# Value gate folded into a scaled matrix and three LayerNorm chains moved to GpSimd, in an attention and routed-FFN layer

## The reference, cut to what matters

```python
h    = layernorm(x) * (1 + scale_a) + shift_a          # modulation rows from silu(c) @ wmod
q, k, v = h @ Wq.T + bq, h @ Wk.T + bk, h @ Wv.T + bv
p    = softmax(causal(abs(q @ k.T) / 16))
x2   = x + gate_a * (p @ v @ Wo.T + bo)
h2   = layernorm(x2) * (1 + scale_b) + shift_b
tile = argmax routing of h2 over 8 clusters x 8 tiles (sigmoid, piecewise linear in 8 knots)
comp = tanh(gelu(h2 @ w1 + b1) @ w2 + b2)              # 2 numbers per token
mag  = small spline of comp with the parameters of the chosen tile
y    = h2 + mag * directions[tile] * output_scale
out  = x2 + gate_b * (layernorm(y) * gamma + beta)
```

## Time and profile before

| | |
|---|---|
| Median of 3 runs | 475.73 us (473.7 to 475.93) |
| Profiled execution | 474.78 us, span 473.0 us |
| TensorE busy | 403.7 us (85%), 2136 products |
| VectorE busy | 400.6 us (85%), 1367 instructions |
| ScalarE busy | 295.5 us (62%), 645 instructions |
| GpSimd busy | 42.7 us (9%), 64 instructions |
| Mean granted TensorE clock | 0.939 of full |

### The profile page before, as it was taken

How to read it: one execution, slowest core, us unless ns; L and a number is a source line. 1 busy time by engine, 2 the same in 40 slices (tenths; PEclk the granted TensorE clock), 3 DMA queues, 4 the chain that set the end, 5 groups by cost and what they waited for, 6 DMA issues and landing times.

```text
span 473.0 us, 7756 instructions
## 1 busy us (share of the span) xinstructions
PE 403.7 (85%) x2136; PEld 315.1 (67%) x2136; DVE 400.6 (85%) x1367; ACT 295.5 (62%) x645; POOL 42.7 (9%) x64
## 2 busy tenths in 40 slices
PE   2595799999999998999899989998999999963330
PEld 2563568767886886779586858786878787863330
DVE  4436536478799999999999999999999989998986
ACT  2230274949885968597758776797669865772410
POOL 2000003000000022001300040004000400040040
PEclk9879799999999999999999999999999999987565
DMA  8602102100300051104210320024101100110022
GB/s 303 148 2 79 48 1 62 41 11 2 100 2 33 8 161 46 34 2 135 77 35 1 122 91 35 1 59 154 24 1 49 65 24 1 67 46 0 0 90 89
DMA packets 26206, 26.59 MB, mean 56 GB/s; under 512 B 3874, under 2 KB 23588, under 8 KB 26164
## 3 DMA queue, kind: packets, MB, share of 16 engines
q1 hardware_dynamic: 24132, 24.25, 16.1%
q10 hardware_dynamic: 2032, 1.85, 1.2%
HBM read 17.66 MB, written 8.44 MB: 55 GB/s over the span
## 4 chain that ended last, share of the span: by engine, by line
DVE 51%; PE 32%; issue 9%; ACT 4%; ACTq 2%; DVEq 0%
PE bank L476 6%; PE bank L495 6%; PE bank L466 4%; PE bank L453 4%; PE bank L518 3%; DVE x L1043 3%; DVE res L1240 3%; DVE st L998 3%; DVE seg_val L1099 3%; DVE st L1206 3%; DVE val L1102 3%; DVE y L1230 3%; DVE v L1022 3%; DVE probs L1029 3%; DVE st L1049 2%
## 5 line engine op out<-in xcount | busy, mean ns | idle before, releaser
L476 PE MATMUL bank<-h,g 128*128 128x128 f32 (+3 forms) x256 | 80.6, 444 | 8.1 <-DVE v L1022 8.1
L495 PE MATMUL bank<-v,probsT 128*128 128x257 f32 x320 | 80.5, 383 | 0.0
L934 POOL TENSOR_TENSOR res<-x,gb_row 128x512 f32<-128x512 f32 x32 | 40.3, 1279 | 413.7 <-DMA out<-res 339.7
L466 PE MATMUL bank<-m_sb,h 128*128 128x258 f32 x256 | 66.0, 382 | 0.0
L476 PEld LDWEIGHTS bank<-h,g 128*128 128x128 f32 x256 | 44.5, 195 | 27.5 <-issue 11.0
L495 PEld LDWEIGHTS bank<-v,probsT 128*128 128x128 f32 x320 | 56.8, 190 | 8.0 <-issue 1.3
L453 PE MATMUL bank<-h,a_sb 128*128 128x512 f32 x128 | 59.8, 596 | 1.5 <-ACT gath L788 1.4
L466 PEld LDWEIGHTS bank<-m_sb,h 128*128 128x128 f32 x256 | 44.6, 192 | 6.8 <-issue 2.2
L699 ACT ACTIVATE bank<-bank,v 128x128 f32<-128x128 f32 (+1 forms) x64 | 31.6, 494 | 26.8 <-PE bank L476 23.8
L674 ACT ACTIVATE xhat<-x,nmr,rstd 128x256 f32<-128x256 f32 x64 | 36.7, 594 | 15.7 <-DVE nmr L989 15.7
L1029 DVE CUSTOM_DVE_ANT_0 probs<-bank,cmask 128x128 f32<-128x128 f32 (+1 forms) x64 | 31.1, 485 | 12.7 <-ACT bank L699 12.7
(11 more groups left out here) (175 smaller groups left out, 769.7 us busy)
## 6 DMA issues: line engine op xcount, KB each, us to landing
x<-in_L_attn_x SPq DMA_DIRECT2D x16, 512.0 KB, 3.8
out<-res SPq DMA_DIRECT2D x16, 512.0 KB, 3.0
gb_row<-gate_rows SPq DMA_DIRECT2D x16, 256.0 KB, 3.1
ga_row<-gate_rows SPq DMA_DIRECT2D x16, 128.0 KB, 2.9
wide<-in_L_wmod ACTq DMA_DIRECT2D x2, 768.0 KB, 7.3
res<-in_L_attn_Wq SPq DMA_DIRECT2D x1, 256.0 KB, 4.9
res<-in_L_attn_Wk SPq DMA_DIRECT2D x1, 256.0 KB, 7.2
res<-in_L_attn_Wo SPq DMA_DIRECT2D x1, 256.0 KB, 9.8
```

The source lines that it names most:

```text
L466: last = mm(ps[:, 0:VW], h[s][:, c, t * P:(t + 1) * P], m_sb[:, c, :], start=False, stop=(c == KC - 1))
L476: last = mm(ps[:, 0:w], g[s][:, c, t * P:(t + 1) * P], h[s][:, c, 0:w], start=(c == 0), stop=(c == KC - 1))
L495: last = mm(ps[:, 0:D + 1], probsT[s][t][:, j * P:(j + 1) * P], v_sb[s][:, j, 0:D + 1], start=(j == 0), stop=(j == t))
L934: gp.tensor_tensor(res[:, 2 * u:2 * u + 2, :], x2[p % 2][s][:, t, :], gb_row[p % 2][s][:, 1:2, :].broadcast_to([P, 2, D]), ALU.add).then_i ...
```

## The change

The diff has four parts, and it replaces every order list.

1. The value bias product is gone. GpSimd multiplies the folded value matrix by the sequence's gate row, column by column (`ms`, one instruction of 128x512 per sequence), into `m_ga`. `V_` is then the two products of h with `m_ga`. `b_v` adds a row instead of multiplying by one; the row (gate times bias) is computed once on 16 partitions and goes through `gate_rows`, whose rows now hold four parts.
2. The three LayerNorm chains leave VectorE and ScalarE. GpSimd runs `layer_norm`: 14 small instructions, nine of which are followed by a wait on them, with the inverse root by an element-wise power and one Newton step. `a_ln`, `c_ln` and `y_ln` are its three uses. The eight first statistics and the two half chains of pair 0 stay as they were.
3. `a_st` waits until the chain before is through with the statistics; `oa` and `ob` both wait for the end of `y_ln` (before, `oa` needed the mean alone).
4. The orders of all engines are new, with new banks. On TensorE `HD`, `CM`, `OHT`, `GA` and `BT` run one superstep later against the attention of a later pair, and on VectorE the routing is cut at `clc` 3, and `spl`, `y_`, `y_st`, `oa` and `ob` belong to pair k-4. `base` runs for pair k-3.

```diff
+            @step
+            def ms(p, s):
+                if seq(p, s) == 0:
+                    pool.wait_ge(m_rdy, 1)
+                pool.wait_ge(ga_ld[p % 2][s], 16 * (p // 2 + 1))
+                need(pool, v_done, NT * seq(p - 2, s) + NT)
+                gp.tensor_tensor(m_ga[p % 2][s][:, :, 0:D], m_sb[:, :, :],
+                                 a_row[p % 2][s][:, 0:D].unsqueeze(1).broadcast_to([P, KC, D]), ALU.mult).then_inc(ms_rdy, 1)
+
+            def layer_norm(chain, ln, ready):
...
+                chain.mark(tt(dif, st[:, :, 1], st[:, :, 4], ALU.subtract))
+                chain.mark(tt(sums, st[:, :, 1], st[:, :, 4], ALU.add))
+                chain.link(pool, tt(var, st[:, :, 2], st[:, :, 5], ALU.add))
+                chain.mark(ts(var, var, 1.0 / D, EPS, ALU.mult, ALU.add))
+                chain.link(pool, tt(dif, dif, dif, ALU.mult))
+                chain.mark(ts(dif, dif, 0.25, None, ALU.mult))
+                chain.link(pool, ts(nmu, sums, -0.5, None, ALU.mult))
+                chain.link(pool, tt(var, var, dif, ALU.add))
+                chain.link(pool, tt(rstd, var, neg_half[:, :], ALU.pow))
+                chain.link(pool, tt(newt, rstd, rstd, ALU.mult))
+                chain.link(pool, tt(newt, newt, var, ALU.mult))
+                chain.link(pool, ts(newt, newt, -0.5, 1.5, ALU.mult, ALU.add))
+                chain.link(pool, tt(rstd, rstd, newt, ALU.mult))
+                tt(nmr, nmu, rstd, ALU.mult).then_inc(ready, 1)
...
             def superstep(k):
-                for i in range(0, 4):
-                    base(k, i)
...
+                c_ln(k - 2)
+                ms(k, 0)
+                y_ln(k - 4)
+                ms(k, 1)
+                base(k - 3, 0)
+                a_ln(k)
+                for i in range(1, 4):
+                    base(k - 3, i)
```

On TensorE:

```diff
-                mm(ps[:, 0:VW], ones[:, :], vbias[:, :], start=True, stop=False)
                 for c in range(KC):
-                    last = mm(ps[:, 0:VW], h[s][:, c, t * P:(t + 1) * P], m_sb[:, c, :], start=False, stop=(c == KC - 1))
+                    last = mm(ps[:, 0:VW], h[s][:, c, t * P:(t + 1) * P], m_ga[p % 2][s][:, c, :],
+                              start=(c == 0), stop=(c == KC - 1))
...
             def superstep(k):
...
+                AT(k - 2, 1, 3)
+                HD(k - 3)
                 for i in range(0, 2):
+                    V_(k - 1, 0, i)
+                BT(k - 4, 3)
                 for i in range(0, 2):
                     G_(k - 1, 0, i)
                 for i in range(2, 4):
                     V_(k - 1, 0, i)
+                CM(k - 3)
+                for i in range(0, 2):
                     HT(k - 2, i)
                 S_(k - 1, 0, 0)
```

On ScalarE:

```diff
             def superstep(k):
+                for i in range(0, 7):
+                    c_xh(k - 2, i)
+                for i in range(0, 2):
+                    b_g(k - 1, 0, i)
+                c_xh(k - 2, 7)
+                for i in range(0, 2):
+                    c_h2(k - 2, i)
+                b_abs(k - 1, 0, 0)
                 for i in range(2, 4):
                     c_h2(k - 2, i)
...
+                a_h(k - 1, 1, 0)
+                tanh(k - 3)
+                b_exp(k - 1, 0, 0)
```

More of the change, by code:

```diff
@@ L816, in _ @@
             first_half(1)
-            ahead.add(("a_gs", 0, ()))
             act.wait_ge(bias_rdy, 1)
@@ new lines, in _, with a_ln, c_ln @@
+            ahead.add(("a_ln", 0, ()))
+            @step
+            def a_ln(p):
+                pool_ln1.at(p - 1)
+                pool.wait_ge(st1_rdy, PT * p)
+                need(pool, xhat_ready, PT * p)
+                layer_norm(pool_ln1, ln1, ln1_ready)
+            @step
+            def c_ln(p):
+                pool_ln2.at(p)
+                pool.wait_ge(st2_rdy, PT * (p + 1))
+                need(pool, xhat2_rdy, PT * p)
+                layer_norm(pool_ln2, ln2, ln2_ready)
@@ L928, in base, with y_ln @@
+            @step
+            def y_ln(p):
+                pool_ln3.at(p)
+                pool.wait_ge(st3_rdy, PT * (p + 1))
+                need(pool, res_rdy, PT * p)
+                layer_norm(pool_ln3, ln3, ln3_ready)
             @step
@@ L1225, in oa @@
                 if t == 0:
[L1226 to L1227 removed]
+                    dve.wait_ge(ln3_ready, p + 1)
                 if t % NT == 0:
@@ new lines, in superstep @@
+                clc(k - 3, 10)
+                spl(k - 4, 2)
+                clc(k - 3, 11)
+                spl(k - 4, 3)
+                clb(k - 3, 0)
+                b_st(k - 2, 0, 0)
+                spl(k - 4, 4)
+                clb(k - 3, 1)
+                spl(k - 4, 5)
+                clb(k - 3, 2)
+                b_ttr(k - 2, 0, 3)
+                y_(k - 4, 0)
+                clb(k - 3, 3)
+                y_(k - 4, 1)
+                clb(k - 3, 4)
+                y_(k - 4, 2)
```

582 lines of the change are left out of this document (259 added, 323 removed), and 16 rows, old and new, of the table BANK.

## The result

The changed kernel takes 513.57 us (median of 4 runs, 512.14 to 516.04), the kernel before 475.51 on the same chip: a ratio of 1.0813, 95% interval 1.0771 to 1.0856. The forecast was 484.3, in a range of 467 to 504. The direction was right, the size was not. The profiled execution took 512.14, with a span of 510.3.

A forecast was written before the change was run, and what follows sets the result against it. VectorE was taken to pace the middle at 49.3 us per pair, TensorE close behind at 46.0 to 46.4. Head 79.7, middle 326 and tail 76.8 gave 482.5, plus 1.8: 484.3 us, range 467 to 504.

The forecast's parts named there:

- The tail: From pair 7's last AT to the end: 76.8 us, 19 more, of which about 6 is L and 13 the deeper pipeline.
- 2.0 us of port waits: Routing's second half in the tail: VectorE held because base of pair 6 comes in the middle.
- VectorE's 2.1 us: Kernel before: two VectorE instructions lasting 1.27 and 1.19 us instead of 0.17 beside GpSimd's base additions, per pair.
- The other two chains: GpSimd's y_ln and a_ln: both cost nothing at L = 4.5 and about 1 us each at 7.
- L: Length of a GpSimd LayerNorm chain of 14 instructions: 4.5 us, against some 2.3 now from statistics to output.
- the middle: From the last AT of pair 0 to that of pair 7: 326 us, against 334.8 before.
- the forecast's cover for y_ln: y_ln ends about when VectorE comes to oa, because b_ttr waits there anyway; without it, 2 us per pair.
- It fits VectorE's side: Check of the middle: VectorE needs 308 us with 4.6 of contention, within TensorE's 326.
- my 48.1: VectorE's need per full pair in us: 43.5 plus 4.6 of contention, range 43.5 to 52.5.
- the forecast's own formula: TensorE's stall per pair at the first S, waiting for g behind c_ln: L - 3.3, or 1.2 us.
- The bias product: Removing it from TensorE: 0.12 us each, eight per pair, so 1.0 us per pair (46.0 to 45.0).
- C: Rival, long chain: power or linked instruction dearer, L = 7, stalls 4.8 us per pair, 511 us; chance 0.12.

The follow-up runs named there:

- run without the power: Changed kernel with the element-wise power replaced by a same-shape multiplication in all three LayerNorm chains; 504.17 us.
- g first: Changed kernel with ScalarE's two b_g copies ahead of the eight c_xh, and HT 1 moved to bank 0; 512.27 us.
- a_ln first: Changed kernel with GpSimd's a_ln chain put ahead of the first base addition instead of behind it; 519.14 us.
- made small: Changed kernel with the four base additions cut from 256 to 4 columns per tile; 498.13 us.
- short chains: Changed kernel with each 14-instruction LayerNorm chain cut to three unlinked instructions, 474.51 us; also with four-column additions, 457.66, and in the mended kernel, 466.65.
- both orders: Changed kernel with both b_g ahead of the c_xh, HT 1's bank moved, and a_ln ahead of the first base addition; 503.86 us.
- mended kernel: Changed kernel with both orders mended and the last three base additions of a pair held until its first y; 493.58 us.
- fastest kernel: Kernel before with the gated value matrix, no bias product, and base additions and gate multiplications held back beside VectorE's y; 462.05 us.

## Why the prediction was wrong

**Read rightly.** The tail: 78.2 against 76.8, with the routing at 19.4 us from the last AT (forecast 17.6), picked at 32, onehot's end at 42.6 (42.0), spline at 52.8 (52.0). The rows, shifted step by step through the new order, were enough for its shape. That its steps met so well is partly luck: the first half of the routing began 1.8 us late and ended 3.7 late (32.2 against 28.5), as the additions held VectorE there, and the second half, where I had put the 2.0 us of port waits, took 10.4 instead of 13.5. A linked small instruction is 0.28 to 0.30 us (0.3). VectorE's 2.1 us read off two rows of before are what one wait gave back. The Trainium skill's page "SBUF — State Buffer" ("Who interferes with whom") says that a VectorE instruction with at most one SBUF input, outside certain faster modes, does not contend with GpSimd, and that one with two contends with a GpSimd instruction that reads SBUF; both halves are seen here, 0.41 us for v beside the additions and 1.33 in place of 0.23 beside the multiplications.

**The step that failed first: "The other two chains ... Both cost nothing at L = 4.5 and about 1 us each at 7."** The run without the power has c_ln at 4.59 us, and it still took 504.17, 19.9 above the forecast, with full pairs of 50.9 to 53.7 us. Its y_ln takes 4.2 us, its a_ln 5.4, as VectorE holds two of its instructions. The chain of that run goes through just these two, y_ln - output - send - base 0 - a_ln - a_xh - g - scores product, and TensorE waits 2.0 us at its end. I had looked at a_ln's slack with base 0 where it was then, and at y_ln's with VectorE where it was then. But base 0 is timed by a send that is timed by y_ln, and all three chains and the gated matrix share one in-order queue, so GpSimd closes a loop through VectorE and TensorE once per pair.

In the changed kernel itself this loop stands just behind another, through c_ln: c_ln - c_xh and g - HT 1 - TensorE - VectorE's routing - the scores and AT of TensorE - c_ln. Its chain that ended last passes through c_ln in every pair of the middle from pair 1 on and never through y_ln or a_ln. There the forecast's cover for y_ln held, by 0.1 us: y_ln ended at 292.53, and VectorE stood until 292.63 for the first b_ttr. Two loops of nearly one length account for the pattern of the runs: g first shortens the one through c_ln and meets the other, a_ln first shortens the other and leaves the first, and only both together give something. By how much a microsecond on either loop lengthens a pair is not shown. It is not simply one for one, since the full pairs without the power are as long as those with it, and in them VectorE is busy for up to 48.2 us instead of up to 47.5.

**The second step that failed: "It fits VectorE's side".** I let VectorE's contention vanish under TensorE's time in the middle. The four additions alone take 4.0 us of VectorE per full pair (46.0 and 47.5 against 41.9 and 43.7), where I had 4 x 0.6 = 2.4, and made small they give back 8.6 us of the middle and 5.0 of the tail; with short chains, 12.0 of the middle (330.2 against 318.2). They lie on the chain between TensorE's products (the rows at 308.75 to 310.96). That VectorE's busy time came out under my 48.1 in all, at 46.0 to 47.5, hid this.

**Mis-sized, with the right mechanism.** L was 6.05 for c_ln in a full pair instead of 4.5: 1.1 more for the power (1.68 against 0.6), 1.0 for the two instructions held by VectorE, and 0.5 less because instructions that are not joined start 0.17 us apart. At 0.41 us of time per power the power accounts for 9.4 us. With L = 6.05 the forecast's own formula gives 2.75 us (L - 3.3) at the end of c_ln's path; TensorE waits 0.98 + 1.33 = 2.31 there. So this stall came about as the formula says, only at HT and not at the first S: the bank of HT 1 was in the diff, and I hadn't read it as a wait, and that is the 1.33. Behind it TensorE waits 1.05 at the second sequence's S and 0.78 after that, where I had 0.8 in all.

The full pairs put together: the forecast has 45.0 of products, 0.4 of gaps and 2.0 of stall, 47.4 us, and 51.8 and 53.1 were measured. TensorE's idle time is 4.0 and 4.1 instead of 2.4 (1.6 and 1.7). Its busy time at clock 1.00 is 46.4, in the runs with g first and with both orders, not 45.0 (1.4). The rest, 1.5 and 2.5, goes with the lower clock of these two pairs, 0.97 and 0.94.

**Not priced at all.** What a short wait does to the clock. The forecast took waits at face value. Behind the two waits at HT the granted clock was 0.62 over 4.5 us, and TensorE's busy time is 47.8 and 48.9 us per pair instead of the 46.4 of the run at clock 1.00 with the same products.

**Too small to matter.** The bias product: I took 1.0 us per pair off TensorE and put all of it into the middle. It shows as 0.6 where TensorE alone sets the pace, and as nothing in the kernel before, where VectorE does.

**The rivals.** C (511) comes nearest to the time, and its condition was met halfway: the power was long, the linked instruction was not, and L came to 6.05 and not to 7. With L = 6.05 its formula gives a middle of about 337 (309 + 3 + 7 x 3.55) and a tail of about 81, some 500 us in all, so its nearness is in part luck. The prediction also prices the other two chains in two ways, at about 1 us each at L = 7 where it names the step, and at 0.3 together in C. What is left over the formula, the second loop, the additions on the chain and the clock, lay in none of the rivals.

**What stays open.** The mended kernel with full chains (493.58) is 19.9 us above the kernel before beside it (473.68). 26.9 us are chain length, but how they divide between the loop through y_ln and TensorE's waits at HT (19.3 us in all 15 waits there, the first of 7.9) was not told apart. That g first alone lost from the third pair on just what it had won in the first two is laid to the loop as read from the chain, and to the pair of runs that opened it; no run takes y_ln or a_ln alone out of it. What decides the clock behind a wait of 2.0 us (0.66 in one run, 1.00 in another) is open as well. What the new orders and the later stages cost by themselves was not run apart either: with short chains the mended kernel's tail is still 63.1 against the 54.9 of the fastest kernel, which has its LayerNorms.

## What to carry to other kernels

When work moves to an idle engine, write down that engine's new queue and ask of each entry what it waits for, and who waits for the entry behind it. Look for a loop that comes back to the same queue within one iteration: the slack of its entries cannot be read one by one, and a share of idle time (GpSimd 66% idle here) says nothing. When two such loops are nearly equal, mending one shows no gain until the other is mended too. And before moving anything, look at what the engine's present instructions run beside: one wait that shifted four additions next to instructions with at most one SBUF input was worth about 2% (ratio 0.9785).

## What the runs showed of the hardware

- An element-wise power on GpSimd takes 1.67 us for 128 x 8 numbers, a product of the same shape 0.20. Small instructions joined by a wait on the engine's own semaphore start 0.28 to 0.30 us apart, those not joined 0.17.
- Beside a GpSimd instruction that reads two SBUF tiles (1.25 us), a VectorE instruction with two SBUF inputs takes up to 1.1 us longer, for few columns as for many: 0.17 became 1.27 for 8, 0.23 became 1.33 for 64, 0.62 became 1.59 for 448. Beside the same GpSimd instruction v, with one input in PSUM, keeps its 0.41. GpSimd is held too: 0.96 instead of 0.20 beside a VectorE product of 896 columns.
- Two waits of 1.0 and 1.3 us close together were followed by a granted clock of 0.62; one of 2.04 us by 0.66, but one of 2.01 at the same product by 1.00; one wait of 1.0 and one of 0.46, with g already there, by 1.00, and the kernel before's waits of 1.72 by 1.00.
